# Macaron block, attention: row maxima turned ahead of the value products, tile 0's stack loaded in two parts, context product on GpSimd

## The reference

```python
# parameters as fixed by the inputs: x is (8, 512, 128) float32
def attn(x, wq, bq, wk, bk, wv, bv, wo, bo, gamma, beta):        # B=8, S=512, E=128, 16 heads of 8
    Q = (x @ wq + bq).reshape(B * 16, S, 8)
    K = (x @ wk + bk).reshape(B * 16, S, 8)
    V = (x @ wv + bv).reshape(B * 16, S, 8)
    scores = jnp.einsum('bqd,bkd->bqk', Q, K) / jnp.sqrt(jnp.float32(8))
    attn = jax.nn.softmax(scores, axis=-1)
    ctx = jnp.einsum('bqk,bkd->bqd', attn, V).reshape(B, S, E)
    out = ctx @ wo + bo + x
    mu, var = jnp.mean(out, -1, keepdims=True), jnp.var(out, -1, keepdims=True)
    return (out - mu) * jax.lax.rsqrt(var + 1e-5) * gamma + beta

def moe(x, router_w, w_gate, w_up, w_down, ws_gate_up, ws_down):  # 64 experts, 8 per token
    probs = jax.nn.softmax(x @ router_w.T, axis=-1)
    topk_w, topk_ids = jax.lax.top_k(probs, 8)                    # weights normalised to sum 1
    ...                                                           # at most 64 slots per expert
    y = (silu(xb @ w_gate) * (xb @ w_up)) @ w_down                # per expert, then weighted sum
    return routed + silu(x @ ws_gu[:, :96]) * (x @ ws_gu[:, 96:]) @ ws_down

x = x + 0.5 * moe(layernorm(x))
x = x + attn(layernorm(x))
x = x + 0.5 * moe(layernorm(x))
```

## Time and profile before

| what | before |
|---|---|
| median of 3 runs | 839.35 us |
| the profiled execution | 840.47 us |
| its span (first to last instruction) | 838.9 us |
| granted TensorE clock, mean | 0.846 |
| busy: TensorE / VectorE / ScalarE / GpSimd | 649.3 / 615.5 / 461.0 / 393.9 us |
| first scores begin (L1701) | at 208.63 us of the span |
| first attention step begins | at 227.6 us |
| last attention step ends | at about 655 us |

### The profile page before, as it was taken

One profiled execution on the slowest core, in us unless ns is written; L12 is line 12 of the kernel. 1 busy time (PEld: TensorE's weight loads), 2 busy tenths in 40 slices (PEclk: granted clock), 3 DMA queues, 4 the chain that ended last, 5 costly groups with the idle time before them and its releaser, 6 DMA issues.

```text
span 838.9 us, 16313 instructions
## 1 busy us (share of the span) xinstructions
PE 649.3 (77%) x5121; PEld 283.2 (34%) x5121; DVE 615.5 (73%) x1580; ACT 461.0 (55%) x1057; POOL 393.9 (47%) x529
## 2 busy tenths in 40 slices
PE   4895677612699999999999999999998777675760
PEld 3643455411222222222222222222223534443440
DVE  4788733456968889889898898998983879843430
ACT  5753222200277778787778778877878644222220
POOL 5575778754523324243343433343301448578762
PEclk9997655765589999999999999999999768757565
DMA  7997444336434444454544444444421212544334
GB/s 197 238 261 198 90 73 63 52 45 131 94 86 97 117 102 107 106 113 107 113 108 101 115 103 103 120 99 123 98 77 35 61 38 73 124 84 68 57 42 113
DMA packets 242983, 86.66 MB, mean 103 GB/s; under 512 B 169992, under 2 KB 235688, under 8 KB 242856
## 3 DMA queue, kind: packets, MB, share of 16 engines
q1 hardware_dynamic: 225928, 72.95, 36.2%
q0 software_dynamic: 12288, 10.49, 8.4%
q10 hardware_dynamic: 4704, 2.49, 1.1%
HBM read 56.23 MB, written 31.49 MB: 105 GB/s over the span
## 4 chain that ended last, share of the span: by engine, by line
PE 42%; issue 13%; ACT 13%; POOL 13%; DVE 11%; DMA 6%; SPq 1%; ACTq 0%; POOLq 0%; DVEq 0%
PE psum L1723 14%; PE psum L1714 11%; ACT arena L1429 9%; POOL sums L678 7%; PE psum L1701 4%; POOL arena L653 4%; PE psum L1668 3%; DMA sums<-sums_sb,sidx 3%; DVE arena L1098 2%; DMA arena<-dispatch_rows,arena 1%; PE psum L1691 1%; PE psum L1509 1%; DVE arena L915 1%; PE psum L1596 1%; PE psum L1677 1%
## 5 line engine op out<-in xcount | busy, mean ns | idle before, releaser
L1098 DVE TENSOR_REDUCE arena<-psum 128x2 f32<-128x1024 f32 x256 | 308.2, 1217 | 45.2 <-PE psum L1703 44.1
L1429 ACT ACTIVATE arena<-psum 128x512 f32<-128x512 f32 x512 | 281.1, 597 | 86.9 <-PE psum L1714 86.0
L1714 PE MATMUL psum<-arena 122*128 122x512 bf16 x512 | 169.9, 388 | 10.7 <-ACT arena L1429 8.1
L1723 PE MATMUL psum<-arena 128*32 128x512 f32 x1024 | 136.5, 605 | 0.0
L678 POOL DMA_INDIRECT sums<-sums_sb,sidx x64 | 101.8, 1591 | 44.1 <-issue 17.1
L745 POOL CAST arena<-arena 128x256 bf16<-128x256 f32 x30 | 11.9, 396 | 201.8 <-issue 188.7
L1701 PE MATMUL psum<-arena 48*128 48x512 bf16 x256 | 89.1, 401 | 15.8 <-DMA arena<-qk_parts 9.2
L1703 PE MATMUL psum<-arena 48*128 48x512 bf16 x256 | 89.1, 401 | 0.0
L1714 PEld LDWEIGHTS psum<-arena 122*128 122x128 bf16 x512 | 44.5, 100 | 131.9 <-ACT arena L1429 124.1
L653 POOL DMA_INDIRECT arena<-dispatch_rows,arena x64 | 64.2, 1004 | 27.9 <-issue 17.9
L1586 PE MATMUL psum<-ident,arena 128*128 128x128 f32 x64 | 25.2, 413 | 60.8 <-DMA arena<-dispatch_rows,arena 60.7
(11 more groups left out here) (151 smaller groups left out, 1160.2 us busy)
## 6 DMA issues: line engine op xcount, KB each, us to landing
ctx<-arena SPq DMA_DIRECT2D x32, 256.0 KB, 2.1
arena<-qk_parts SPq DMA_DIRECT2D x126, 64.0 KB
qk_parts<-arena SPq DMA_DIRECT2D x32, 192.0 KB, 3.8
arena<-qk_parts SPq DMA_DIRECT2D x63, 96.0 KB
arena<-qk_parts SPq DMA_DIRECT2D x189, 32.0 KB
arena<-lists SPq DMA_DIRECT2D x16, 256.0 KB, 3.5
sums<-x_sb SPq DMA_DIRECT2D x16, 256.0 KB, 4.2
arena<-ctx SPq DMA_DIRECT2D x64, 64.0 KB, 2.4
```

Of the source, the lines that this page charges most:

```text
L1098: dve.tensor_reduce(mx_r[r % 2][:, p:p + 9:8], src, X, ALU.max).then_inc(a_mx, 1)
L1429: act.activation(p_r[tau % NPB], bank[4 + tau % 2][:, :], ACT.Exp, scale=SCALE).then_inc(a_P, 1)
L1714: pe.matmul(bank[4 + tau % 2][:, :], keys, heads(q_st[r], rows, g), start=True, stop=True)\
L1723: ins = pe.matmul(bank[6][32 * g:32 * g + 32, :], v_r[r][:, g, kt, :], p_r[(4 * kt + g) % NPB], start=(kt == 0), stop=(kt == 3), tile_posi ...
```

## The change

On TensorE and ScalarE, within a step: `maxT` of tile n+1 is issued behind `scores_t` of tau 3 and in front of the first `pv`, where before it stood behind tau 4; `max_copy` follows the exponential of tau 3 and stands ahead of `ctx_copy`, where before it followed tau 5; `xT_copy` follows the exponential of tau 1 and not of tau 0. The order of use of bank 7 stays the same.

VectorE keeps the reciprocal of `ctx_div`. The product of numerators and reciprocals is done by GpSimd (`context`), in front of the next `split`, with a wait for the reciprocal; for the last two tiles VectorE still does it.

Tile 0's loads are issued in two parts. The first scores of tile 0 wait for 12 transfers instead of 16; the other four, for rows 48 to 63 and 112 to 119, are all issued by SyncE behind the store of tile 1's parts and are waited for at the second scores of tile 0.

The rows of -1 under the keys are set as 32-bit words that hold two bf16 values each. The declarations of the two new semaphores are left out of the diff.

```diff
--- before.py
+++ after.py
@@ -47,6 +47,7 @@
     SCALE = float(HD) ** -0.5
+    MINUS_ONES = -(1.0 + 0x3F80 * 2.0 ** -23 + 2.0 ** -8)
     LN_EPS = 1e-5
@@ -464,6 +467,8 @@
                         n = (last - first) * HD
+                        if isinstance(t, int) and t == 0 and row >= LR:
+                            continue
                         sp.dma_start(q_st[r][row:row + n, :], parts[first * HD:last * HD]).then_inc(a_stk[r], 16)
@@ -503,9 +508,18 @@
                 sp.wait_ge(s_kini, 1)
-                for t in range(2):
-                    stack_store(t, t)
-                    stack_load(t, t)
+                def first_rest():
+                    parts = parts_dram[0].rearrange("g c (d j) s -> (c d) g (j s)", d=HD)
+                    for first, last, row in PAIRS[3:]:
+                        n, src = (last - first) * HD, NPART * HD
+                        sp.dma_start(q_st[0][row:row + n, :], parts[first * HD:last * HD]).then_inc(a_late, 16)
+                        sp.dma_start(k_st[0][row:row + n, :], parts[src:src + n]).then_inc(a_late, 16)
+
+                stack_store(0, 0)
+                stack_load(0, 0)
+                stack_store(1, 1)
+                first_rest()
+                stack_load(1, 1)
                 stack_store(2, 2)
@@ -764,11 +778,17 @@
                     pool.tensor_tensor(z, z, gamma_sb[:].unsqueeze(1).to_broadcast([P, len(ts), P]), ALU.mult).then_inc(a_fin1, 1)
+                def context(t, r):
+                    pool.wait_ge(a_rc, t + 1)
+                    wait(pool, a_use, use("o", t - 2) + 1 if not isinstance(t, int) or t >= 2 else 0)
+                    pool.tensor_tensor(cT_r[r % 2], num_r[r % 2], den2_r[r % 2], ALU.mult).then_inc(a_ct, 1)
                 split(2, 2)
...
                     n = t - 4
+                    if n >= 2:
+                        context(n - 2, (n - 2) % NBUF)
                     split(t, t % NBUF)
@@ -779,8 +799,12 @@
                 f = ffns[1]
+                for t in range(NT - 6, NT - 4):
+                    context(t, t % NBUF)
                 z_rstd(6)
+                context(NT - 4, (NT - 4) % NBUF)
                 z_gamma(6)
+                context(NT - 3, (NT - 3) % NBUF)
                 route_weights(f, 0, 0)
@@ -1065,7 +1089,7 @@
                 for i in range(NBUF):
-                    dve.memset(k_st[i][3 * P // 4:P, :], -1.0).then_inc(s_kset, 1)
+                    dve.memset(k_st[i][3 * P // 4:P, :].bitcast(F32), MINUS_ONES).then_inc(s_kset, 1)
                     dve.memset(q_st[i][CR:ER, QC // 2:QC], 0.0).then_inc(s_kset, 1)
@@ -1109,9 +1133,11 @@
                     dve.reciprocal(den2_r[r % 2], den2_r[r % 2]).then_inc(a_rc, 1)
+                    if t < NT - 2:
+                        return
                     dve.wait_ge(a_rc, t + 1)
-                    wait(dve, a_use, use("o", t - 2) + 1 if not isinstance(t, int) or t >= 2 else 0)
-                    dve.tensor_tensor(cT_r[r % 2], num_r[r % 2], den2_r[r % 2], ALU.mult).then_inc(a_ct, 1)
+                    wait(dve, a_use, use("o", t - 2) + 1)
+                    dve.tensor_tensor(cT_r[r % 2], num_r[r % 2], den2_r[r % 2], ALU.mult).then_inc(a_ctl, 1)
 
@@ -1404,13 +1430,11 @@
                     parts = parts_dram[0].rearrange("g c (d j) s -> (c d) g (j s)", d=HD)
-                    for first, last, row in PAIRS:
-                        n = (last - first) * HD
-                        src = (2 * NPART - last) * HD if first == 0 else NPART * HD
+                    for first, last, row in PAIRS[0:3]:
+                        n, src = (last - first) * HD, (2 * NPART - last) * HD
                         act.dma_start(k_st[0][row:row + n, :], parts[src:src + n]).then_inc(a_stk[0], 16)
-                        if row < LR:
-                            act.dma_start(k_st[0][CR + row:CR + row + n, QC // 2:QC], parts[src:src + n, NH // 2:NH, :])\
-                               .then_inc(a_stk[0], 16)
+                        act.dma_start(k_st[0][CR + row:CR + row + n, QC // 2:QC], parts[src:src + n, NH // 2:NH, :])\
+                           .then_inc(a_stk[0], 16)
 
@@ -1427,12 +1451,12 @@
                         act.activation(p_r[tau % NPB], bank[4 + tau % 2][:, :], ACT.Exp, scale=SCALE).then_inc(a_P, 1)
-                        if tau == 0 and n + 4 < NT:
+                        if tau == 1 and n + 4 < NT:
                             xT_copy(n + 4, r)
+                        if tau == 3 and n + 1 < NT:
+                            max_copy(n + 1, (r + 1) % NBUF)
                         if tau == 3 and n >= 1:
                             ctx_copy(n - 1, (r - 1) % NBUF)
-                        if tau == 5 and n + 1 < NT:
-                            max_copy(n + 1, (r + 1) % NBUF)
                         if tau == 7 and n + 4 < NT:
@@ -1686,7 +1710,10 @@
                 def proj(t, r):
-                    pe.wait_ge(a_ct, t + 1)
+                    if isinstance(t, int) and t >= NT - 2:
+                        pe.wait_ge(a_ctl, t - (NT - 3))
+                    else:
+                        pe.wait_ge(a_ct, t + 1)
                     misc("o", t)
@@ -1694,7 +1721,7 @@
                     if p == 0:
-                        pe.wait_ge(a_stk[r], lap(t, r, NBUF, 16 * 16))
+                        pe.wait_ge(a_stk[r], lap(t, r, NBUF, 16 * 16) - (16 * 4 if r == 0 else 0))
                     wait(pe, a_mx, 8 * t + (p - 1))
@@ -1708,6 +1735,8 @@
                         pe.wait_ge(a_mrow[r], lap(t, r, NBUF, 16))
+                    if tau == 0 and isinstance(t, int) and t == 0:
+                        pe.wait_ge(a_late, 16 * 4)
                     wait(pe, a_P, 16 * t + (tau - 1))
@@ -1730,8 +1759,6 @@
                             xT(n + 4, r)
-                        if tau == 5 and (mid or n + 1 < end):
-                            maxT(n + 1, at(1))
                         if tau == 6 and (mid or n + 4 < end):
@@ -1746,6 +1773,8 @@
                         scores_t(n, r, tau)
+                        if tau == 3 and (mid or n + 1 < end):
+                            maxT(n + 1, at(1))
                         if tau == 3 and (mid or n >= 1):
```

2 lines of the change are left out of this document (added).

## The result

The changed kernel takes **816.76 us**, the median of 4 runs (815.09 to 817.6), against 840.51 us (839.17 to 841.9, 4 runs) for the kernel before on the same chip: ratio 0.9715, 95% interval 0.9688 to 0.9742. The forecast was 824.4 us, with a range of 819 to 832. The direction is right, and the size is not: the gain is 23.8 us and not 15.0.

The account below looks back on a forecast made before the run. TensorE, busy 56.79 of 60 us, was taken to bound the attention, with VectorE's chain limiting the gain. Steps 13.0 us plus start 2.0 made 15.0 us, forecasting 824.4 us against a median of 839.35; range 819 to 832.

Parts of the forecast that it names:

- xT_copy: On ScalarE, behind the exponential of tau 1: second scores of tau 3 start 0.15 us earlier.
- maxT: On TensorE, ahead of the value products: still costs 0.16 us there; everything behind its old place comes 0.16 us earlier.
- max_copy: On ScalarE, ahead of the context copy: fits into 0.43 us of idling; `qk` loses its 0.48 us wait.
- The product on GpSimd and VectorE's chain: Product leaves VectorE, hidden on GpSimd; VectorE's chain ends last, so a step gains 0.49 us.
- The six steps behind the long product: Steps behind GpSimd's long product: earlier scores do not help VectorE there, so only 0.33 us each is won.
- The start: Tile 0's first scores wait for 12 loads, not 16: 2.0 us, bounds 0.7 and 3.3.
- The memsets: Words of -1 at the attention's start: VectorE done up to 3.5 us earlier, hidden by the token reload; gain nothing.
- TensorE keeps all 0.64: Rival: VectorE does not hold TensorE, each step gains 0.64 us; 819.4 us; chance 0.12.
- The lock: Rival: GpSimd's product holds VectorE up 0.45 us every step, which gains 0.04; 835.7 us; chance 0.12.
- The waits did not just change their name: Rival: something unseen sets the step at 13.2 us, only the start gains; 837.4 us; chance 0.05.
- The slower rival: TensorE waits at `maxT` for a late `max_low`; loses from 0.62 us a step; 844.1 us at 0.8; chance 0.05.

Follow-up runs that it names:

- e4: Changed kernel with the copy of the transposed x back behind the exponential of tau 0: 818.84 us.
- e10: Changed kernel with the transposition of the maxima back between the second scores of tau 4 and 5, its copy behind the exponential of tau 4: 822.28 us.
- e9: Changed kernel with only the copy of the maxima back behind the exponential of tau 5: 833.98 us.
- e3: Changed kernel with the product of numerators and reciprocals back on VectorE for all tiles: 823.76 us.
- e8: Changed kernel with the reciprocal one place later, behind the fourth pair of maxima instead of the third: 810.52 us.
- e2: Changed kernel with the transposition of the maxima directly behind the value products and its copy directly behind the context's copy: 814.69 us.
- e6: Changed kernel with the words of -1 set as 2048 bf16 values again: 817.91 us.
- e7: Changed kernel with GpSimd doing the context product twice, first into a tile nobody reads: 819.27 us.
- e11: Changed kernel with reciprocal behind the fourth maxima, transposition of the maxima behind the value products and its copy behind the context's: 814.95 us.
- e12: Changed kernel with the reciprocal behind the fifth pair of maxima instead of the third: 831.53 us.
- e1: Changed kernel with both the transposition and the copy of the maxima back in their old places: 827.27 us.
- e5: Changed kernel with tile 0's 16 loads waited for as a whole, in the old order of issue: 815.81 us.

## Why the prediction was wrong in size, point by point

**xT_copy: right.** 0.15 us was forecast, and 0.17 measured (e4). The wait before tau 3 is down to 0.10 us.

**maxT: the step that failed.** The prediction had it cost "0.16 us of TensorE's time, now in front of the first value products instead of behind them", a length taken from a row of the chain, and so had the third pair of first scores only 0.16 us earlier. That is one price for two places, and both are off. In front of the value products it costs 0.01 us there (e4's rows against the earlier trace rows) and 0.02 at the next second scores, between two second scores 0.25 to 0.26 (e10). So the third pair gains 0.17 + 0.25 = 0.42 us (4.02 to 3.60), and not 0.16. The share of an instruction in the chain says how long the chain leant on it, not what its neighbours would do without it. The Trainium skill (TensorE: Matmul & The Clock Gate, Part 3: Packing small matmuls) says that small products on different tiles of the array, such as columns whose outputs lie on different groups of 32 partitions, run concurrently. The four value products of a group do so (2.21 to 2.23 us into the step before). The transposition, whose output is 32 partitions wide too, starts 0.01 us ahead of them: 495.32 and 495.33. Its output lies on the same partitions of its bank as the first value product's in its own, so the page's words do not cover this pair; the rows do.

**max_copy: right.** The copy fits into ScalarE's idle time, and `qk` follows the scores at once. The move is worth more than the wait that it removes: with the copy late, nothing that TensorE wins ahead of it arrives (e9).

**The product on GpSimd and VectorE's chain: right.** From third to sixth pair 0.33 us less was forecast; 0.38 was measured, by e3 and by the two traces (4.03 to 3.65). The other 0.05 us lie in the last link: the maxima behind the reciprocal take 1.16 us in the changed kernel's trace, where they took 1.22. 0.42 + 0.38 = 0.80 us, the whole gain of a plain step, where the prediction had 0.16 + 0.33 = 0.49. TensorE's wait at the sixth pair was to grow to about 0.27 us, and is 0.29. That VectorE's chain binds is shown by e8, which takes the reciprocal out of it and wins that wait back.

**The six steps behind the long product: the forecast was wrong, and the difference agrees by luck.** They were to gain 0.33 us, 0.16 less than the others. They gain 13.42 - 12.78 = 0.64, again 0.16 less than the others, but not for the reason given. VectorE is busy nearly without a pause in the whole of such a step (0.14 us of idling before, 0.07 after), and 0.66 us lie on its path: the third maxima start 4.33 us into the step instead of 4.45, so 0.12 of the earlier scores does help; from these to the fourth it is 0.34 less, the product; and from the fourth to the fifth 0.21 less, of which 0.15 is the sum with x between them (L1156, then L1182), 0.82 us before and 0.67 after. The prediction did not have this last term, and why the sum is shorter no run tests. Beyond the 0.12, scores that come earlier do not help: with the third pair at 3.62 (e2) or 3.85 us (e10) into such a step it takes 12.78 us all the same, and e4's take no longer either. The collision of `max_low` with GpSimd's product is still there, and has used up the 0.1 us of air at the transposition:

```profile
569.75 1.27 DVE L1130 TENSOR_TENSOR arena<-arena 128x16 bf16<-128x16 f32 x1
```

```profile
569.07 0.33 PE L1687 MATMUL psum<-ident,arena 128*128 128x128 f32 x1
...
571.15 0.23 PE L1710 MATMUL psum<-identb,arena 128*32 128x128 bf16 x1
571.26 1.06 PE L1752 MATMUL psum<-arena 128*32 128x512 f32 x8
```

`max_low` ends at 571.02, and the value products start 2.19 us into the step instead of 2.05. The steps next to them (13.70 to 12.98) gain 0.72; I had not told these apart from the plain ones.

**The start: within its bounds, a little high.** 2.0 us was the middle between 0.7 and 3.3; the two traces differ by 1.35, and the twelve traces with the parted loads (33.98 to 34.88) lie 1.4 to 2.3 us below the two without (36.23, 36.25). The upper bound let the load land in 2.03 us; none landed in less than 3.65.

**The memsets: right for the changed kernel, not in general.** They are done early there, VectorE waits 2.77 us for the reload, and the statistics start 3.0 us after the reload's issue, as before. But before, VectorE and the reload ended within 0.02 us of each other, and in e6 the old words made VectorE last by 1.1 us. So the gain is 0 to about 1 us, as the execution falls, and not nothing.

**Not forecast:** the stretch behind the last second scores is 1.4 us longer. TensorE's clock there, by stretches, before and after:

```profile
642.00:657.00 15.00, 11.91 (x78) 4.97 (x74) 8.90 (x40) 12.36 (x32) 2.56 (x3) 1.00 0.15 37
657.00:672.00 15.00, 12.24 (x57) 10.30 (x58) 11.44 (x73) 9.18 (x27) 9.03 (x15) 0.59 0.28 70
```

```profile
620.00:635.00 15.00, 10.80 (x67) 4.24 (x65) 9.23 (x48) 10.62 (x28) 3.94 (x8) 0.97 0.15 37
635.00:650.00 15.00, 13.32 (x58) 10.49 (x57) 10.47 (x66) 9.28 (x27) 7.73 (x13) 0.50 0.28 70
```

It fell to the 1.2 GHz level 4.5 us after the start of the last two second scores, at the end of an idle time of 2.89 us; before, it fell 6.4 us after, 1.6 us behind the same idle time. The fourteen kernels sort by this: where the clock fell within 3.6 to 4.8 us (after, e4, e6, e7, e9, e11, e12), the stretch takes 29.2 to 29.3 us; where it fell after 5.8 to 6.7 us (before, e1, e2, e3, e8, e10), 27.7 to 28.4; and where it fell only after some 14 us (e5), 27.4. No part of the change goes with it. What decides when the clock falls stays open.

**The sum.** Steps 2 to 26 gained 18.7 us, the first two 0.7, the last 1.8 and the start 1.4, less the 1.4 behind them: 21.1 us in the attention, of the 23.8 between the medians. The other 2.7 are of the size by which code that is the same scatters here. The steps together were to gain 13.0 and gained 21.2. What was missed is 0.31 us a step, 0.26 at `maxT` and 0.05 in the last link of VectorE's chain; over 26 steps that is 8.1 us.

**The rivals.** "TensorE keeps all 0.64" is out, since VectorE holds the sixth pair; its 819.4 us was nearest only by the size of the number. The lock is out: the maxima beside GpSimd's product take 2.37 us for two, as with none beside them (2.36, e8), and of the 200 maxima in steps 2 to 26 none takes more than 1.23 us. Where two instructions do collide is seen at `max_low`, and at VectorE's copy L1100 above, 1.91 us for two beside GpSimd's clearing of a tile (182.08 to 184.47), 0.46 before, without it. The Trainium skill (SBUF — State Buffer, on the shared port pair) has such a copy hold the pair that GpSimd uses, and the reduction not; the trace agrees. The Trainium skill's warning (Perfetto Trace Analysis, Optimizing Scalar/DVE Operations) that such a move might not help did not hold for a reduction from PSUM: 0.38 us a step. The waits did not just change their name. The slower rival needed 0.62 us a step at `maxT`, which stands at 2.04 us into a plain step and at 2.08 behind the long product, 0.04 us late; e12 shows that GpSimd could have brought about such an end, by another way than the one I named.

## What to carry to other kernels

Price a moved instruction by its neighbours in the old place and in the new one, not by its own length: look in the trace how far apart the neighbours stand with and without such a thing between them. When a wait is split over two engines, move both halves or neither: here the transposition alone gave nothing, and the copy alone, moved by one exponential, half. And when work moves to an engine with air, follow what stands behind it on that engine to the next thing that the bound engine needs: a late input uses up the air as much as a long instruction does. Last, compare stretches of the trace and not only totals: here a trace of the same code differs by 4 us ahead of the attention.

## What the runs showed of the hardware

- A transposition with a 32-wide output moves value products of 32 columns behind it by 0.01 us (495.32 and 495.33; e4: 0.33 against 0.32 us), and the full-size product behind the group by 0.02 us in front of the group and 0.04 behind it (3.06 and 3.08 against 3.04). Between two second scores of 122x128 by 512 it costs 0.25 to 0.26 us (e10: 0.48 from one to the next against 0.23).
- The load that tile 0's scores wait for landed 3.65 to 4.65 us after its issue with 12 loads in the air (twelve traces), and 4.63 and 4.33 us with 16: most of the saving lay in the earlier issue.
- Maxima of 128x1024 from PSUM take 1.16 to 1.23 us with or without a GpSimd instruction beside them (200 in the changed kernel's trace).
